# Attention scores of a two-layer transformer kernel: bf16 products of three parts against fp32 products in 32-row groups

## The chip, the core and the metric

The kernel runs on one core of a Trainium2 chip. The metric is the device time of one execution in microseconds (us). The engines are TensorE (PE in the profile, its weight loads PEld), VectorE (DVE), ScalarE (ACT), GpSimd (POOL) and SyncE (SP, which only issues DMAs here).

## The reference

1024 tokens of width 256 pass through two layers. Each layer is an attention and a mixture of experts, each with a LayerNorm ahead and behind and a residual. The change touches the two attentions alone (16 heads of width 16, causal):

```
q = x Wq (+ bq)    k = x Wk (+ bk)    v = x Wv (+ bv)      # the biases in layer 0; rotary q, k in layer 1
scores = q k^T * 16 ** -0.5 ;  scores[t, s] = -inf for s > t
y = softmax(scores) v ;  out = y Wo (+ bo)
```

The softmax subtracts from each row of scores its maximum, in the reference and in both kernels.

## The kernel before

Everything of the attention stays in SBUF. Queries are handled in two chunks of 512 tokens and keys in blocks of 128; heads go in four groups of four. For each layer the work goes so:

- **Head.** LayerNorm, transposes, then the projections (L624) give q and k as fp32 in X, transposed (channels on partitions). Scores need about fp32 accuracy, so each of q and k is split into three bf16 parts (L900 on ACT, L234 on DVE or POOL). SP copies them with 56 DMAs over both layers (L410), 16 rows at a time, to QA and KA: seven stacked products of 16 rows make 112 rows for each head. Rotary (layer 1) runs ahead of the split on DVE and POOL (L1116 to L1119, L536). The values (L635, with the bias as a product of one row, L638) go to V.
- **Maxima.** A *max unit* is a bank of PSUM with scores with queries on partitions: a bf16 product of 112 rows (L658), on the diagonal with a product of the constants `identb` and `mask_q` (L661) added to its last 128 columns, which puts -1e30 above the diagonal. DVE takes the maxima (L1134). Units of 128 columns hold four heads and those of 256 two. They use three banks in turn (`ps`, `RB = 3`), and a unit waits until DVE has emptied the bank (`unit_out`).
- **Rows.** The negated maxima in two bf16 parts (`nb`) are turned by TensorE (L667), copied by ACT (L941) and put by DMA into rows 112 and 113 of QA, against ones in KA. KA's ones come from a POOL memset (L524) at the start of each layer.
- **Scores.** 48 *steps* for each layer (group, query chunk, key block): four products with keys on partitions (L687, two heads for each ACT instruction), the exponential on ACT (L922), POOL's causal mask on diagonal blocks (L555), and *weigh*, four fp32 products with V side by side in 32 columns of the array each (L703). *Turn* turns the result (L673), DVE divides (L1151, L1152).

`schedule()` writes the order of units, scores and weighs by hand, and PE, ACT and DVE all follow it: each group's units stand between the scores of the group ahead. PE takes its instructions in that order.

Of the kernel before, what the change touches and what calls it, by code (L numbers as in the profile page):

```python
# [14 lines left out]
P = 128  # L15
# [21 lines left out]
Q_PARTS = (0, 0, 0, 1, 1, 1, 2)  # L37
K_PARTS = (0, 1, 2, 0, 1, 2, 0)
HM = H // KD
NPROD = 7  # L40
KQ = NPROD * DH
NSH = 2
KX = KQ + NSH
ONES_AT = KQ // 32 * 32

# [36 lines left out]
def max_units():  # L82


    units = []
    for i in range(NT):
        if i >= TPC:
            units += [(0, i, hh, 1, 0, CH) for hh in range(HG)]
# [3 lines left out]
    return units  # L92


MAX_UNITS = max_units()
NMAX = len(MAX_UNITS)
CHUNK_UNITS = [sum(u[1] < TPC * (c + 1) for u in MAX_UNITS) for c in range(NC)]
RB = 3
PB = 3

OWN_RATE, NEXT_RATE = 4, (5, 4, 4, 4)
OWN_AHEAD, NEXT_AHEAD = 10, 10
ROWS_AT = (6, NSTEP - 2)


def schedule():

    rest = [("max", 0, u) for u in range(CHUNK_UNITS[0], NMAX)] + [("rows", 0, 1)]
    out = [("max", 0, u) for u in range(CHUNK_UNITS[0])] + [("rows", 0, 0)] + rest[:OWN_AHEAD]
    rest = rest[OWN_AHEAD:]
    last = NG * NSTEP
    for st in range(last + 2):
        g, s = divmod(st, NSTEP)  # L120
        if s == 0 and g + 1 < NG:
            nxt = [("max", g + 1, u) for u in range(NMAX)]
        more = []
        if g == 0 and s < TPC:
            more = rest[:OWN_RATE]
            rest = rest[OWN_RATE:]
            if s == TPC - 1:
                more += rest + nxt[:NEXT_AHEAD]
                nxt = nxt[NEXT_AHEAD:]
        elif g + 1 < NG:  # L130
            more = nxt[:NEXT_RATE[g]]
            nxt = nxt[len(more):]
        if g + 1 < NG:

            for c in range(NC):
                if s == ROWS_AT[c]:
                    more.append(("rows", g + 1, c))
        if s == TPC + 3 and g < NG:
            more.append(("turn", NC * g))
        if s == 3 and 0 < g < NG:  # L140
            more.append(("turn", NC * g - 1))
# [7 lines left out]
        out += more  # L149
    return out + [("turn", NC * NG - 1)]  # L150


SCHEDULE = schedule()
UNITS = [x for x in SCHEDULE if x[0] in ("max", "rows", "turn")]
UNIT_NO = {x: n for n, x in enumerate(UNITS)}

EMPTIED = [sum(y[0] != "rows" for y in UNITS[:n + 1]) for n in range(len(UNITS))]
ROWS_DONE = [sum(y[0] == "rows" for y in UNITS[:n + 1]) for n in range(len(UNITS))]

# [17 lines left out]


DVE_PARTS = ((0, 0), (0, 1))
POOL_PARTS = ((1, 0), (1, 1))  # L180
# [29 lines left out]
def build(nc, a, out):  # L210
    ctx = ExitStack()
    with ctx:
# [7 lines left out]
        def left(L, m, j, part):  # L220

            who, those = ("pool", POOL_PARTS) if (m, j) in POOL_PARTS else ("dve", DVE_PARTS)
            return S(f"left{part}_{who}"), len(those) * L + those.index((m, j)) + 1

        def max_rows(eng, L, g, c):
            for j in range(NSH):
                eng.dma_start(QA[KQ + j:KQ + j + 1, HG * g:HG * (g + 1), c * CH:(c + 1) * CH],
                              mT[HG * j:HG * (j + 1), c * CH:(c + 1) * CH]).then_inc(S(f"max_rows{L}_{c}"), 16)

        def take_part(eng, L, m, j, part):  # L230

            eng.wait_ge(S(f"parts_p{part}_{L}"), 2 * m + j + 1)
            q = qkf[:, j, m, :]
            eng.tensor_tensor(q if part == 1 else parts[:, j, m, 2, :], q, parts[:, j, m, part - 1, :], ALU.subtract)\  # L234
               .then_inc(left(L, m, j, part)[0], 1)

# [14 lines left out]
        identb = sb("identb", [P, P], BF16)  # L251
        mask_q = sb("mask_q", [P, P], BF16)
# [25 lines left out]
        QA = sb("QA", [P, H, T], BF16)  # L278
        KA = sb("KA", [P, H, T], BF16)
        X = sb("X", [P, 10240])  # L280

        qkf = X[:, 0:4096].rearrange("p (a m t) -> p a m t", a=2, m=KD)
        parts = X[:, 4096:10240].bitcast(BF16).rearrange("p (a m r t) -> p a m r t", a=2, m=KD, r=PARTS)
# [4 lines left out]
        swapped = V[:, :, :, :].rearrange("p a b c -> p (a b c)")[:, 0:2 * T].rearrange("p (a t) -> p a t", a=2)  # L288
        by_cos = V[:, :, :, :].rearrange("p a b c -> p (a b c)")[:, 2 * T:4 * T].rearrange("p (a t) -> p a t", a=2)
        rden = sb("rden", [P, 2, TPC, HG])  # L290
        mx = sb("mx", [P, 2, NT, HG])
        nb = sb("nb", [P, NT, NSH, HG], BF16)
        mT = sb("mT", [NSH * HG, T], BF16)

# [55 lines left out]
        def _(sp):  # L350
# [42 lines left out]
            for L in range(2):  # L393
# [38 lines left out]
                if L == 0:  # L432
                    zero_sums(0)
                    zero_sums(1)


                rest = INTER[L] - P

# [1001 lines left out]
```

## Time and profile before

| what | us |
|---|---|
| median of three runs | 1030.9 (1030.26 to 1034.15) |
| span of the profiled execution, first to last instruction | 1058.4 |
| layer 0: first projection to first score | 28.46 to 110.15 |
| layer 0: first score to last turn | 110.15 to 239.84 |
| layer 1: first projection to first score | 594.75 to 677.39 |
| layer 1: first score to last turn | 677.39 to 807.54 |

The profiled execution is known by its span alone; it is 27.5 us above the median. Rows are read so: a mean in ns is from the start of one instruction to its end, and matmuls overlap, so the time that one really adds is the distance of the starts. An fp32 product is recorded as two passes, so a row "x8" can be four products.

### The profile page before, as it was taken

The page shows a single profiled execution, that of the slowest core. Times are in us where ns is not written, and L with a number is a line of the kernel's source. Part 1 is how long each engine was busy: PE and PEld are TensorE (multiplying, and loading weights), DVE is VectorE, ACT ScalarE, POOL GpSimd, SP SyncE. Part 2 cuts the span into 40 slices and gives each one's busy share as a digit, 9 for nine tenths or more (in the row PEclk, how much of TensorE's full clock was granted, in tenths as well). Part 3 has the DMA queues.
Part 4 walks back from the last instruction along what each step waited for, and adds up shares of the span by engine and source line. Part 5 has one row for each costly group of instructions (what it writes and reads, how often), then busy time and mean ns, then how long its engine had stood idle before and what let it go on. Part 6 is the DMA issues. An engine that isn't in the chain of part 4 may idle for free.

```text
span 1058.4 us, 14617 instructions
## 1 busy us (share of the span) xinstructions
PE 754.7 (71%) x4353; PEld 439.7 (42%) x4353; DVE 494.6 (47%) x1442; ACT 330.7 (31%) x660; POOL 336.4 (32%) x371
## 2 busy tenths in 40 slices
PE   0930899996753889999881632589998496899970
PEld 0510334423521667666660321134434443576650
DVE  7211977804630344444444762587742740144444
ACT  1500366682200222222220340246674320032221
POOL 6210011120075255555457150001110047035560
PEclk9965899999575899999995776799999598899995
DMA  2599053480052799999997099300000111089974
GB/s 74 60 115 103 2 167 103 147 264 1 1 177 77 227 246 261 270 260 262 247 231 212 2 118 119 40 12 2 2 1 22 67 48 41 24 235 264 263 178 129
DMA packets 88634, 134.28 MB, mean 127 GB/s; under 512 B 9883, under 2 KB 67082, under 8 KB 88464
## 3 DMA queue, kind: packets, MB, share of 16 engines
q1 hardware_dynamic: 57808, 101.31, 38.0%
q0 software_dynamic: 16896, 19.37, 10.6%
q10 hardware_dynamic: 13888, 13.06, 4.4%
q8 instruction: 24, 0.39, 0.2%
q14 instruction: 18, 0.15, 0.1%
HBM read 80.74 MB, written 40.06 MB: 114 GB/s over the span
## 4 chain that ended last, share of the span: by engine, by line
PE 29%; DVE 18%; POOL 14%; issue 14%; DMA 11%; another core or an unknown queue 5%; SPq 4%; ACT 4%; POOLq 0%; ACTq 0%; DVEq 0%
POOL acc L578 12%; DVE mx L1134 7%; DMA KA<-X 6%; PE ps L703 5%; PE ps L687 5%; PE ps L764 4%; SPq L410 4%; PE ps L658 4%; DMA acc<-X,token 3%; PE ps L798 2%; PE ps L605 2%; POOL pause L576 2%; ACT X L922 1%; PE ps L732 1%
## 5 line engine op out<-in xcount | busy, mean ns | idle before, releaser
L1134 DVE TENSOR_REDUCE mx<-ps 128x1 f32<-128x512 f32 (+3 forms) x304 | 180.2, 657 | 128.1 <-PE ps L661 76.7
L658 PE MATMUL ps<-KA,QA 112*128 112x512 bf16 (+3 forms) x384 | 116.7, 355 | 85.6 <-ACT mT L941 44.1
L922 ACT ACTIVATE X<-ps 128x1024 f32<-128x1024 f32 (+1 forms) x192 | 146.2, 811 | 84.9 <-PE ps L687 84.3
L578 POOL DMA_INDIRECT acc<-X,token x96 | 149.8, 1561 | 15.1 <-issue 14.9
L821 PE MATMUL ps<-X,KA 128*128 128x128 f32 x1152 | 149.3, 280 | 1.4 <-DMA KA<-in_ex 0.8
L821 PEld LDWEIGHTS ps<-X,KA 128*128 128x128 f32 x1152 | 139.6, 196 | 4.3 <-issue 2.9
L555 POOL TENSOR_SCALAR_AFFINE_SELECT X<-X 128x512 f32<-128x512 f32 x64 | 40.8, 637 | 311.2 <-ACT X L922 311.2
L1337 DVE TENSOR_SCALAR X<-ps,egate 128x256 f32<-128x256 f32 x96 | 46.5, 484 | 145.5 <-DMA acc<-X,token 145.0
L566 POOL DMA_INDIRECT slot_rows<-xn,slot_i x64 | 64.8, 1013 | 127.2 <-issue 73.7
L658 PEld LDWEIGHTS ps<-KA,QA 112*128 112x128 bf16 x384 | 37.4, 103 | 157.4 <-DVE mx L1134 50.8
L990 ACT ACTIVATE X<-ps 128x256 f32<-128x256 f32 x96 | 36.9, 385 | 201.9 <-DVE token L1311 84.2
L687 PE MATMUL ps<-QA,KA 114*128 114x512 bf16 (+3 forms) x384 | 92.7, 327 | 3.7 <-ACT X L922 3.4
L703 PE MATMUL ps<-X,V 128*32 128x512 f32 (+3 forms) x768 | 81.1, 497 | 0.4 <-ACT X L930 0.4
L605 PE MATMUL ps<-identf,xn 128*128 128x128 f32 x64 | 14.5, 415 | 89.1 <-ACT xn L866 72.3
L831 PE MATMUL ps<-KA,X 128*128 128x256 f32 x192 | 61.9, 404 | 22.3 <-DVE X L1326 10.3
L576 POOL TENSOR_TENSOR pause<-empty 128x1 f32<-128x1 f32 x96 | 20.1, 209 | 178.4 <-DVE X L1337 178.3
L764 PE MATMUL ps<-xT,w_sgu 128*128 128x512 f32 x112 | 59.5, 693 | 16.2 <-DVE QA L1221 8.2
L833 PE MATMUL ps<-KA,X 64*128 64x256 f32 (+1 forms) x192 | 67.6, 432 | 0.0
L798 PE MATMUL ps<-w_sdn,QA 128*128 128x256 f32 (+1 forms) x128 | 42.3, 474 | 25.8 <-issue 18.2
L661 PE MATMUL ps<-mask_q,identb 128*128 128x128 bf16 x256 | 54.7, 238 | 0.0
L605 PEld LDWEIGHTS ps<-identf,xn 128*128 128x128 f32 x64 | 12.7, 221 | 90.7 <-ACT xn L866 50.6
L687 PEld LDWEIGHTS ps<-QA,KA 114*128 114x128 bf16 x384 | 29.6, 98 | 48.3 <-ACT X L922 23.5
(174 smaller groups left out, 934.3 us busy)
## 6 DMA issues: line engine op xcount, KB each, us to landing
KA<-in_ex SPq DMA_DIRECT2D x96, 512.0 KB
slot_rows<-empty SPq DMA_DIRECT2D x12, 1060.0 KB, 10.1
X<-slot_rows ACTq DMA_DIRECT2D x96, 132.5 KB
QA<-X SPq DMA_DIRECT2D x28, 256.0 KB, 23.1
KA<-X SPq DMA_DIRECT2D x28, 256.0 KB, 25.4
KA<-in_dn SPq DMA_DIRECT2D x64, 64.0 KB
X<-acc SPq DMA_DIRECT2D x8, 512.0 KB, 6.6
acc<-empty SPq DMA_DIRECT2D x2, 1152.0 KB, 10.4
```

Source lines behind the costliest of these rows:

```text
L566: pool.indirect_dma_start(out=slot_rows[L], out_offset=bass.IndirectOffsetOnAxis(ap=slot_i[:, n:n + 1], axis=0), in_=xn[:, i, :], in_offse ...
L578: pool.indirect_dma_start(out=acc[L][r % 2], out_offset=bass.IndirectOffsetOnAxis(ap=token[:, r:r + 1], axis=0), in_=erows[:, r % 2, :], i ...
L658: mm = pe.matmul(ps[:, bank, j * w:(j + 1) * w], QA[0:KQ, h, i * P:(i + 1) * P], KA[0:KQ, h, s0:s0 + w], start=True, stop=not diag)
L687: mm = pe.matmul(ps[:, 4 + 2 * p + x, off:CH], KA[0:KX, h, b * P:(b + 1) * P], QA[0:KX, h, c * CH + off:(c + 1) * CH], start=True, stop=True)
L703: mm = pe.matmul(ps[32 * x:32 * x + 32, RB, off:CH], V[:, b, HG * g + x, :], probs[:, st % PB, x, off:CH], start=(b == 0), stop=(b == TPC ...
L764: mm = pe.matmul(ps[:, 2 * (u % 2) + x, :], w_sgu[:, k, col:col + P], xT[:, k, n * CH:(n + 1) * CH], start=(k == 0), stop=(k == KD - 1))
L798: mm = pe.matmul(ps[:, 6 + i % 2, 0:D], actv[0:rows_j, j, i * P:(i + 1) * P], w_sdn[0:rows_j, j, :], start=(j == 0), stop=(j == nsc - 1))
L821: mm = pe.matmul(ps[:, 2 + r % 2, m * P:(m + 1) * P], w_ex[:, r, col:col + P], rowsT[:, r % 2, k, :], start=(k == 0), stop=(k == KD - 1))
L831: pe.matmul(ps[:, 4 + r % 2, 0:D], eact[:, r % 2, 0:P], w_ex[:, r, KD * UPC * P:EW], start=True, stop=False)
L833: mm = pe.matmul(ps[:, 4 + r % 2, 0:D], eact[0:erest, r % 2, P:2 * P], w_rest[0:erest, r, :], start=False, stop=True)
L922: nc.scalar.activation(probs[:, st % PB, 2 * p:2 * p + 2, off:CH], ps[:, 4 + 2 * p:6 + 2 * p, off:CH], ACT.Exp, scale=SCALE).then_inc(S(f" ...
L1134: v.tensor_reduce(mx[:, part, i, h0:h0 + nh], ps[:, n % RB, 0:nh * w].rearrange("p (h w) -> p h w", h=nh), AX.X, ALU.max)\
```

## The change

- q and k are kept as fp32 in `QT` and `KT` (one buffer, QK), one plane for each group of four heads: head h of a group sits in partitions 32h to 32h+15. The weights' columns are arranged so that the projection puts group 2m into place; ACT writes k multiplied by a 0/1 column (`half`), with ones in the unused rows, and group 2m+1 comes from a DVE shuffle of partitions (`shuf`). The three parts, the 56 row copies and the memset of KA are gone.
- Every score is an fp32 product of 16 rows (maxima) or 17 (scores). The negated maximum of each query and head is written by DVE into `shifts`, TensorE turns it, and DVE adds it to row 16 of each head in QT (`rows`); the two DMAs for each of these are gone.
- A max unit now holds one head: 192 for each layer. Units come in pairs (heads 0,1 or 2,3), and a pair stands behind the score pair of the two other heads. On the diagonal the bf16 mask product of all 128 rows follows each unit's product. DVE takes plain maxima, one for each unit.
- Projections of the later heads and the values stand between the first group's max units. Layer 1's rotary is done in eight pieces of 512 columns.
- SP issues layer 0's later loads and the clearing of HBM at the start. POOL clears `shifts` and V's padding at the start.

The core of the diff:

```diff
-        w = (i % TPC + 1) * P
-        n = {1: 4, 2: 2, 3: 1, 4: 1}[w // P]
-        units += [(1, i, hh, n, (i // TPC) * CH, w) for hh in range(0, HG, n)]
+    for i in range(TPC * c, TPC * (c + 1)):
+        out += [(i, s0, CH) for s0 in range(0, CH * c, CH)] + [(i, CH * c, (i % TPC + 1) * P)]
...
+            out.extend(("max", g, i, 2 * side + x, s0, w) for x in range(2))
...
         for p in range(2):
             if st < last:
                 out.append(("score", st, p))
-            out += more[:1]
-            more = more[1:]
+            take(1 - p)
...
-                sp.wait_ge(S(f"k_ones{L}"), 1)
-                            for r in range(NPROD):
-                                if those[r] == part:
-                                    sp.dma_start(dst[DH * r:DH * (r + 1), HM * m:HM * (m + 1), :],
-                                                 parts[:, j, m, part, :]).then_inc(S(f"qa_rows{L}_{m}"), 16)
...
-                pool.memset(KA[ONES_AT:KX, :, :], 1.0).then_inc(S(f"k_ones{L}"), 1)
...
-                            mm = pe.matmul(ps[:, bank, j * w:(j + 1) * w], QA[0:KQ, h, i * P:(i + 1) * P],
-                                           KA[0:KQ, h, s0:s0 + w], start=True, stop=not diag)
-                            if diag:
-                                mm = pe.matmul(ps[:, bank, (j + 1) * w - P:(j + 1) * w], identb[:, :], mask_q[:, :],
-                                               start=False, stop=True)
+                        at = slice(32 * h, 32 * h + DH)
+                        mm = pe.matmul(ps[:, bank, 0:w], QT[at, g, i * P:(i + 1) * P], KT[at, g, s0:s0 + w],
+                                       start=True, stop=not diag)
+                        if diag:
+                            mm = pe.matmul(ps[:, bank, w - P:w], identb[:, :], mask_q[:, :], start=False, stop=True)
...
-                        mm = pe.matmul(ps[:, 4 + 2 * p + x, off:CH], KA[0:KX, h, b * P:(b + 1) * P],
-                                       QA[0:KX, h, c * CH + off:(c + 1) * CH], start=True, stop=True)
+                        at = slice(32 * (2 * p + x), 32 * (2 * p + x) + KS)
+                        mm = pe.matmul(ps[:, 4 + 2 * p + x, off:CH], KT[at, g, b * P:(b + 1) * P],
+                                       QT[at, g, c * CH + off:(c + 1) * CH], start=True, stop=True)
...
+                            v.tensor_reduce(shifts[:, c, i % TPC, at:at + 1], ps[:, bank, 0:w], AX.X, ALU.max,
+                                            negate=True).then_inc(S(f"unit_out{L}"), 1)
...
+                        v.scalar_tensor_tensor(q, q, half[:, 0:1], ps[:, bank, :], ALU.mult, ALU.add)\
                          .then_inc(S(f"unit_out{L}"), 1)
```

How the order of instructions changes is shown at three places. The first is PE between two weighs in layer 0. Before, L687 is a score product, L658 a max unit, L661 its mask, L703 a weigh:

```order
L687 MATMUL ps<-QA,KA 128x384 [waits exp0]
L687 MATMUL ps<-QA,KA 128x384
L658 MATMUL ps<-KA,QA 128x384 [waits unit_out0]
L661 MATMUL ps<-mask_q,identb 128x128
L687 MATMUL ps<-QA,KA 128x384 [waits exp0]
L687 MATMUL ps<-QA,KA 128x384
L658 MATMUL ps<-KA,QA 128x384 [waits unit_out0]
L661 MATMUL ps<-mask_q,identb 128x128
L703 MATMUL ps<-X,V 32x128 [waits masked0,exp0]
L703 MATMUL ps<-X,V 32x128 x3
```

The changed kernel at such a place, where L655 is a score product, L626 a max unit and L629 its mask:

```order
L655 MATMUL ps<-QK 128x512 [waits exp0]
L655 MATMUL ps<-QK 128x512
L626 MATMUL ps<-QK 128x512 [waits unit_out0]
L629 MATMUL ps<-mask_q,identb 128x128
L626 MATMUL ps<-QK 128x512 [waits unit_out0]
L629 MATMUL ps<-mask_q,identb 128x128
L655 MATMUL ps<-QK 128x512 [waits exp0]
L655 MATMUL ps<-QK 128x512
L626 MATMUL ps<-QK 128x384 [waits unit_out0]
L629 MATMUL ps<-mask_q,identb 128x128
L626 MATMUL ps<-QK 128x384 [waits unit_out0]
L629 MATMUL ps<-mask_q,identb 128x128
```

Two units, each with its own mask, now stand behind every score pair, where one stood. The second place is PE at the end of layer 0's head before; L635 and L638 are the values:

```order
L635 MATMUL ps<-w_qkv,xT 128x256 [waits qk_sb0]
L635 MATMUL ps<-w_qkv,xT 128x256
L638 MATMUL ps<-bias_v,ones_row 128x256
L658 MATMUL ps<-KA,QA 128x128 [waits qa_rows0_0]
L661 MATMUL ps<-mask_q,identb 128x128
```

And the changed kernel; L604 is a projection, L610 and L613 are the values:

```order
L604 MATMUL ps<-xT,w_qkv 128x512 [waits xT_dve]
L604 MATMUL ps<-xT,w_qkv 128x512 x3
L626 MATMUL ps<-QK 128x128 [waits head_sb0]
L629 MATMUL ps<-mask_q,identb 128x128
L626 MATMUL ps<-QK 128x128
L629 MATMUL ps<-mask_q,identb 128x128
L610 MATMUL ps<-w_qkv,xT 128x256 [waits head_sb0]
L610 MATMUL ps<-w_qkv,xT 128x256
L613 MATMUL ps<-bias_v,ones_row 128x256
```

The first unit waited for the row copies (`qa_rows0_0`) behind all projections and values; now it waits for an ACT result (`head_sb0`) and stands ahead of the values. The third place is POOL at the start. Before:

```order
L509 AFFINE_SELECT before<-before 128x128
L513 AFFINE_SELECT upto<-upto 32x32 x2
L516 MEMSET empty 128x1 [waits pool_own]
L524 MEMSET KA 18x16384 [waits consts]
L234 TENSOR_TENSOR X<-X 128x1024 [waits parts_p1_0,k_ones0]
```

The changed kernel:

```order
L498 MEMSET V 128x128
L500 AFFINE_SELECT before<-before 128x128
L504 AFFINE_SELECT upto<-upto 32x32 x2
L507 MEMSET pause 128x4 [waits pool_own]
L530 AFFINE_SELECT X<-X 128x4x128 [waits exp0,consts]
```

The memset of KA and POOL's share of the splitting are gone.

## Rows read from the trace of the kernel before

**Rows 1.** The page: busy time of the engines, and the chain that ended last.
```profile
PE 754.7 (71%) x4353; PEld 439.7 (42%) x4353; DVE 494.6 (47%) x1442; ACT 330.7 (31%) x660; POOL 336.4 (32%) x371
...
PE 29%; DVE 18%; POOL 14%; issue 14%; DMA 11%; another core or an unknown queue 5%; SPq 4%; ACT 4%; POOLq 0%; ACTq 0%; DVEq 0%
```

**Rows 2.** Windows, core 0: stretch, length, busy (count) by engine, clock, DMA share, GB/s.
```profile
28.46:110.15 81.69, 40.13 (x138) 19.52 (x138) 16.93 (x27) 16.20 (x25) 10.33 (x6) 0.71 0.82 90
110.15:239.84 129.69, 119.81 (x906) 47.15 (x904) 85.78 (x166) 80.41 (x111) 20.38 (x32) 0.99 0.46 139
594.75:677.39 82.64, 33.95 (x122) 18.61 (x121) 39.78 (x43) 16.76 (x26) 20.79 (x10) 0.71 0.80 89
677.39:807.54 130.15, 120.17 (x906) 47.63 (x904) 85.87 (x166) 80.41 (x111) 20.38 (x32) 0.99 0.01 4
213.00:239.84 26.84, 24.02 (x192) 7.22 (x192) 1.36 (x4) 21.05 (x31) 5.73 (x9) 1.00 0.85 261
```

**Rows 3.** Timeline at the start: start, length, engine, line, operation, tiles, count.
```profile
5.01 13.75 POOL L524 MEMSET KA<- 18x16384 bf16 x1
...
6.17 12.62 DVE L1045 TENSOR_SCALAR rs_sq<-mv 128x4 f32<-128x4 f32 x1
...
28.46 15.24 PE L624 MATMUL ps<-xT,w_qkv 128*128 128x512 f32 x32
```

**Rows 4.** Timeline of PE in layer 0's head, then the chain, then the first score.
```profile
45.12 1.13 PE L635 MATMUL ps<-w_qkv,xT 128*128 128x256 f32 x4
46.19 0.69 PE L638 MATMUL ps<-bias_v,ones_row 1*128 1x256 f32 x2
46.81 1.13 PE L635 MATMUL ps<-w_qkv,xT 128*128 128x256 f32 x4
...
72.40 32.81 DMA KA<-X
...
110.15 0.60 PE L687 MATMUL ps<-QA,KA 114*128 114x512 bf16 x2
```

**Rows 5.** Timeline of PE in layer 1's head.
```profile
599.47 7.03 PE L624 MATMUL ps<-xT,w_qkv 128*128 128x512 f32 x16
...
642.38 0.29 PE L658 MATMUL ps<-KA,QA 112*128 112x128 bf16 x1 [19.29 <-DMA KA<-X]
```

**Rows 6.** Groups by form: line, operation, shapes, count, busy, mean ns, idle before.
```profile
L1134 DVE TENSOR_REDUCE mx<-ps 128x1 f32<-128x512 f32 x192 | 120.1, 684 | 53.2 <-PE ps L658 51.1 <-PE ps L661 2.1
...
L922 ACT ACTIVATE X<-ps 128x1024 f32<-128x1024 f32 x96 | 93.7, 1026 | 61.6 <-PE ps L687 61.6
...
L661 PE MATMUL ps<-mask_q,identb 128*128 128x128 bf16 x256 | 54.7, 238 | 0.0
...
L1134 DVE TENSOR_REDUCE mx<-ps 128x1 f32<-128x384 f32 x64 | 32.1, 552 | 3.6 <-PE ps L661 3.6
...
L922 ACT ACTIVATE X<-ps 128x256 f32<-128x256 f32 x32 | 11.4, 384 | 10.7 <-PE ps L687 10.5
...
L673 PE MATMUL ps<-identf,X 128*128 128x128 f32 x64 | 10.0, 279 | 2.0 <-ACT X L930 1.6 <-DVE mx L1134 0.4
...
L1119 DVE TENSOR_TENSOR X<-V 128x1024 f32<-128x1024 f32 x4 | 9.0, 2253 | 0.1
...
L1116 DVE STREAM_SHUFFLE V<-X 128x1024 f32<-128x1024 f32 x4 | 5.2, 1304 | 0.0
```

**Rows 7.** Timeline of PE in layer 1's attention.
```profile
702.92 0.22 PE L661 MATMUL ps<-mask_q,identb 128*128 128x128 bf16 x1
703.07 1.06 PE L703 MATMUL ps<-X,V 128*32 128x512 f32 x8
704.07 0.82 PE L658 MATMUL ps<-KA,QA 112*128 112x512 bf16 x3
```

**Rows 8.** Timeline of PE among the experts.
```profile
470.33 0.70 PE L833 MATMUL ps<-KA,X 64*128 64x256 f32 x2
470.95 0.44 PE L809 MATMUL ps<-identf,X 128*128 128x128 f32 x2
```

More of the change, by code:

```diff
@@ L79 @@
 NSTEP = len(STEPS)
[L82 to L88, printed above, removed]
-        w = (i % TPC + 1) * P
-        n = {1: 4, 2: 2, 3: 1, 4: 1}[w // P]
-        units += [(1, i, hh, n, (i // TPC) * CH, w) for hh in range(0, HG, n)]
[L92 to L97, printed above, removed]
+NPROJ = 2 * KD * NC
+NVP = NT // 2
@@ L106, with take, take_behind, take_rows @@
-ROWS_AT = (6, NSTEP - 2)
+AHEAD = 6
+EXTRA = 2
 def schedule():
-    rest = [("max", 0, u) for u in range(CHUNK_UNITS[0], NMAX)] + [("rows", 0, 1)]
-    out = [("max", 0, u) for u in range(CHUNK_UNITS[0])] + [("rows", 0, 0)] + rest[:OWN_AHEAD]
-    rest = rest[OWN_AHEAD:]
+    first, rest = head_items()
+    out = list(first)
+    units = [(g, c, *u) for g in range(NG) for c in range(NC) for u in max_units(c)]
+    of = [sum((a, b) <= (g, c) for a, b, *_ in units) for g in range(NG) for c in range(NC)]
+    at = [0, 0]
+    rows = [0]
+    def take(side):
+        if at[side] < len(units):
+            g, _, i, s0, w = units[at[side]]
+            out.extend(("max", g, i, 2 * side + x, s0, w) for x in range(2))
+            at[side] += 1
+    def take_behind():
+        take(0 if at[0] < at[1] else 1)
+    def take_rows(least=0, beyond=1):
+        while rows[0] < NG * NC and (min(at) >= min(of[rows[0]] + beyond, len(units)) or rows[0] < least):
+            while min(at) < of[rows[0]]:
+                take_behind()
+            out.append(("rows", *divmod(rows[0], NC)))
+            rows[0] += 1
+    out += [("rope", 0), ("kmask", 0), ("rope", 1)]
+    while min(at) < of[0]:
+        take_behind()
+        if sum(at) == 2:
+            out += [("rope", 2), ("kmask", 2)]
+        if sum(at) == 4:
+            out.append(("rope", 3))
+        if rest:
+            out.append(rest.pop(0))
+    out += [("shuf", u) for u in (1, 0, 3, 2)]
+    for _ in range(AHEAD):
+        take_behind()
+    take_rows(1)
@@ L120, in schedule @@
         g, s = divmod(st, NSTEP)
[L121 to L141, printed above, removed]
+        if st < 4:
+            out.append(("rope", 4 + st))
+        if st in (1, 3):
+            out.append(("kmask", 3 + st))
+        if st in (4, 5):
+            out.extend(("shuf", u) for u in ((5, 4) if st == 4 else (7, 6)))
+        if st < last and s in (0, TPC):
+            take_rows(NC * g + (s == TPC) + 1)
         for p in range(2):
@@ L488, in _ @@
                               allow_small_or_imprecise_dtypes=True))
-            for t in (identf, identb, mask_q):
-                ch.step(pool.memset(t[:, :], 0.0))
+            for t in (identf, identb, mask_q, shifts):
+                ch.step(pool.memset(t[:], 0.0))
             for t in (before, ones, ones_row):
@@ L1094, in xT_copy @@
                     v.tensor_copy(xT[:, k, CH:T], ps[:, KD + k, :]).then_inc(S("xT_dve"), 1)
+            for odd in range(2):
+                ch.step(v.memset(half[:, odd:odd + 1], float(odd)))
+            ch.wait()
+            for odd in range(2):
+                for x in range(HG):
+                    v.memset(half[32 * x:32 * x + DH, odd:odd + 1], float(1 - odd)).then_inc(S("half"), 1)
             halves = (list(range(0, TPC)), list(range(TPC, NT)))
@@ L1126, in _ @@
[L1126 removed]
+                if L == 0:
+                    dve.wait_ge(S("consts"), 1)
+                    dve.wait_ge(S("half"), 2 * HG)
+                    dve.wait_ge(S("bias_qkv"), 32)
+                    ch.link(v.tensor_scalar(k_bias[:, 0, :], bias_qk[:, 1, :], half[:, 0:1], half[:, 1:2], ALU.mult, ALU.add))
+                    v.tensor_scalar(k_bias[:, 1, :], bias_qk[:, 1, :], half[:, 1:2], half[:, 0:1], ALU.mult, ALU.add)\
+                     .then_inc(S("k_bias"), 1)
```

427 lines of the change are left out of this document (211 added, 216 removed).

## The prediction, made before the changed kernel ran

> **What bounds the kernel now.** I read the windows first. From the first score to the last turn each layer takes 130 us, and PE is busy 120 of them, DVE 86, ACT 80 [rows 2]: TensorE bounds the loop, and only in its last 27 us, where no max units are left, ACT (21 of 26.8). Ahead of each loop stand 82 us between the first projection and the first score, with PE busy 40 and 34 of them, the DMA engines at 0.8 and the granted clock at 0.71 on average [rows 2]. The chain says why: the row copies hold the first max unit (17 to 19 us of idle) and the first row of maxima (32.81 us) [rows 4, 5]. Third, at the very start a DVE instruction on 4 columns takes 12.62 us and ends when POOL's memset of KA does (5.01 + 13.75) [rows 3]. Over the span PE is busy 71%, and it has the largest share of the chain, 29% [rows 1]. So the change can win in the heads and must pay in the loops. The experts are left as they are; I take nothing there.
>
> **Prices on TensorE.** A bf16 product of 512 columns takes 0.215 (three in 0.82, the last with its drain) and one of 128 columns 0.053 [rows 7]. An fp32 product runs as two passes of 0.43 (16 passes in 7.03 with the last one's drain) [rows 5]: 0.86 for 512 columns, four times as long. What the change counts on is that products in different parts of the array share this time. In columns they do: four fp32 weighs, eight passes, take 1.00 from start to start of the next work, 0.86 of it streaming [rows 7]. No row shows it for rows of 32; I take the same, pairs and quartets in the time of one.
>
> The other price is the change of the array's layout. From the mask to the weigh is 0.15, of which 0.053 is the mask: 0.10 for the switch; the weigh's 1.00 holds 0.10 for the switch back and 0.03 for weights [rows 7]. Products of 1 or 64 rows show the same for rows, and something more: two passes of 256 columns should take 0.43 and take 0.62, 0.19 more, a switch of 0.10 and a first fp32 weight load of 0.10 that nothing covers [rows 4, 8]. With this in hand the mask is dear: it needs all 128 rows, so behind each product of 16 rows come a switch, the mask, a switch, and an exposed weight load, 0.35 us instead of 0.053. It also parts the two units of a pair, which then don't overlap.
>
> **The loop, for each layer,** counted from the order of the changed kernel (first score onward):
> - Scores: 9 times 512 columns for each head, 16 heads in pairs: 72 x 0.86 = 61.9.
> - Max units on the diagonal: 108, together 69 times 512 columns, one by one: 59.3. Off it 56 in 28 pairs: 24.1.
> - Covered: the unit behind a score pair is on other rows and runs beside it. That is the shorter of the two at 45 diagonal pairs (19.4) and at 21 others (15.1): minus 34.5. Streams: 110.8.
> - Weighs 36 x 0.86 + 48 x 0.03 = 32.4. Masks 108 x 0.053 = 5.7. Switches 299 x 0.096 = 28.7 (96 before). First fp32 loads 132 x 0.10 = 13.2. Turns and rows 15 x 0.5 = 7.5 (four transposes are 0.28 each, overlapped [rows 6], plus a load).
>
> Sum 198. The same count for the kernel before gives 110, and 129.7 were measured: 20 of waits. Waits after: the last 15 steps go exp, score, weigh in a chain (1.03 for a full exp, 0.38 for the narrowest [rows 6], against 0.86 and 0.21 of streaming), 4; a pair of full units off the diagonal occupies DVE 2 x 0.684 [rows 6] with three banks, so the second of the next pair comes late, 28 x 0.4 = 12; the first group's second `rows` is wanted at once by the scores behind it, 3. That is 217. In layer 1 four rotary pieces (a shuffle of 0.65 and two of 1.1, from half of the rows of 1024 columns [rows 6]) stand in DVE's queue in the first steps ahead of the reduces, which PE waits for: 5 more, 222. Against 129.7 and 130.2: **87 + 92 = 179 lost.** The bounds: with all loads covered and no waits but the chain's, 185 in each layer (114 lost); with waits growing as the work does, 240 (220 lost).
>
> DVE has no say in this: plain maxima for one head each cost it, for 128 and 256 columns, about 0.29 and 0.42 (0.552 and 0.684 at 384 and 512 [rows 6], straight on down) instead of a shared 0.69, some 10 us for each layer, and the rows on DVE 8 x 0.7. It is then busy 102 of 217. ACT does less than before.
>
> **The heads.** Layer 0: without the memset the 12.62 is about 0.2, and the first projection starts at 16.5 instead of 28.46; POOL's new clearing of `shifts` and V stands near that DVE instruction but is short (bounds 9 to 12.4 gained). Four projections, partly at the low clock, 8.4; then between the 16 first units the values (8 x 1.69 from start to start [rows 4]) 13.5, four projections 6.9, the units themselves 10 x 0.86 and 16 x 0.35 = 14.2. That is 59.5. DVE's four shuffles and the 12 units ahead (8 x 0.684, 4 x 0.29) 9.2, the turned rows and their addition 1.5: first score at 70 instead of 110.15, **40 gained.** Layer 1: 594.75, rotary of the first keys and queries 9, values 8 x 1.07 [rows 4], 6.9 and 14.2 as above, 1.5 for full banks during a rotary piece, 9.2 and 1.5: first score at 646 instead of 677.39, **31 gained.** SP's loads and clearing that moved to the start stand behind w_qkv in its queue and delay nothing that I see; if they slowed it, by some 5 us, since the first projection comes 12 earlier.
>
> On the memset, the Trainium skill's SBUF — State Buffer (the table's "shared port pair") says that DVE and GpSimd take a port by exclusive lock for a whole instruction; the equal ends in the trace agree. Were it chance, 12 us of the gain would be gone.
>
> **Sum:** 179 - 71 = 108 slower. The profiled execution would go from 1058.4 to 1166; the median of the runs, 27.5 under its span, from 1030.9 to **1139**.
>
> **The rivals.**
> 1. *TensorE goes past the mask.* If a product on other rows could run beside a mask in another bank, with no drain, the row groups would be full: (123.8 + 59.3 + 48.2) / 4 = 58, with 32 + 6 + 7.5 103, and DVE's 102 and its waits would bound: 146 as a loop, 33 lost, 71 gained, 992. For: each waits for banks of its own. Against: the weigh, also in a bank of its own, pays 0.10 on either side [rows 7]. It decides below 165 for a loop. 10%.
> 2. *Row groups share less than column groups.* No row prices it; between full sharing (110.8) and none (231, see 3) I take a quarter of the way, 30 for each layer, 60 in all: 1200. Against: the weigh's 0.86, where four share fully [rows 7]. 12%. A page is for it: the Trainium skill, TensorE: Matmul & The Clock Gate ("Measured speedup vs the span model"), gives 3.07 times for four row tiles of 512 columns. By it the sum would be some 66 more.
> 3. *They don't share at all:* 231 instead of 110.8, 1380. Or the clock stays at its lower level (1.2 of 2.4 GHz) as in the heads before, where PE was idle half of the time [rows 2], though PE is now full: near 1500. Together 9%.
> 4. The sum as it stands, with the bounds above: 1139 + (114 - 179) = 1074 to 1139 + (220 - 179) = 1180. 69%.
>
> **How the numbers follow.** The forecast is rival 4's 1139. The range 1065 to 1215 takes in 4 and 2. Under 0.5% (5 us) a measurement of this kernel can't tell from no change. Rival 1 gives faster (0.10); 0.02 for a loop near 165; the rest, 0.88, is slower.
>
> **What would show it.** In the windows from first score to last turn: 217 and 222 with PE busy nearly throughout, DVE around half. A mask starts 0.10 after the end of its product's passes, and the next product of 16 rows pays 0.20; a score pair and the unit behind it start within a few ns. First scores near 70 and 31 us earlier than now in layer 1's own time; no 12-us DVE instruction at the start. I am wrong if the second unit of a diagonal pair starts beside the first, if a pair takes 2 x 0.86, or if the granted clock falls in the loop.

## The result, and the profile after

The changed kernel takes a median of 1400.9 us (1393.45 to 1424.68), the kernel before 1031.4 (1030.26 to 1034.15) beside it. The ratio is 1.355, with a 95% interval of 1.347 to 1.363. It is slower, as forecast, but by 369.5 us instead of 108, and outside the range. The profiled execution has a span of 1398.9. Single runs of one kernel that lie over 1.5% above its fastest, at a lower granted clock, are left out of every ratio and every comparison here.

The page of the changed kernel: busy time of the engines, PE's and the clock's rows over 40 slices, and the chain that ended last by engine and by line.

```profile
PE 1214.0 (87%) x5121; PEld 580.2 (41%) x5121; DVE 515.9 (37%) x1558; ACT 322.6 (23%) x632; POOL 289.9 (21%) x364
...
PE   6999999999995739898881999999999996899881
...
PEclk9855555555567669999995865555555566899996
...
PE 64%; POOL 12%; issue 11%; DVE 6%; DMA 4%; ACT 2%; POOLq 0%; ACTq 0%; DVEq 0%
PE ps L626 22%; PE ps L655 14%; POOL acc L553 9%; PE ps L671 9%; PE ps L629 4%; PE ps L744 3%; DMA acc<-X,token 2%; PE ps L604 2%; POOL slot_rows L541 2%; PE ps L778 2%; PE ps L610 1%; PE ps L580 1%; POOL pause L551 1%; PE ps L637 1%; PE ps L712 1%
```

PE's share of the chain went from 29% [rows 1] to 64%. The row to see is PEclk: it stands at 5 all through the middle of both loops, in slices in which PE is at 9, while in two slices near 1250 us, among the experts, PE is at 9 as well and the clock is at 9. In its loops TensorE is busy 99% of the time (92% before) and is granted half of its clock. Before, it was the other way round: 0.99 in the full loops and 0.71 in the half idle heads [rows 2].

The windows of the changed kernel: head of layer 0 (first projection to first score), its loop (first score to last turn), and the same for layer 1. Columns as in [rows 2], the clock third from the end.

```profile
16.51:74.37 57.86, 55.54 (x161) 25.17 (x161) 18.52 (x41) 10.92 (x16) 0.00 (x0) 0.85 1.01 276
74.37:420.04 345.67, 342.57 (x1264) 116.71 (x1264) 103.05 (x197) 80.58 (x104) 20.29 (x32) 0.53 0.00 1
769.16:823.52 54.36, 49.81 (x146) 23.90 (x145) 28.36 (x57) 11.25 (x17) 7.83 (x6) 0.85 0.00 0
823.52:1167.12 343.60, 340.63 (x1263) 116.22 (x1264) 110.69 (x212) 83.49 (x108) 22.82 (x34) 0.53 0.00 1
```

Against [rows 2] and [rows 3]: the start gained 12.0, the heads 23.8 and 28.3, and the loops lost 216.0 and 213.5. The rest of the span, almost all of it in code that the change leaves alone, is 24.9 shorter (580.9 for 605.8). That is the difference of 340.5 between the two spans. The 24.9 are the excess of the one profiled execution of before (27.5 above the median): another execution of nearly the same kernel (e8 below) has 580.8 there, as has the changed kernel. They are no gain of the change.

The timeline of PE in the changed kernel, on the diagonal in layer 0.

```profile
202.60 0.80 PE L655 MATMUL ps<-QK 17*128 17x256 f32 x2
202.61 0.79 PE L626 MATMUL ps<-QK 16*128 16x256 f32 x1
203.19 0.64 PE L655 MATMUL ps<-QK 17*128 17x256 f32 x2
203.20 0.63 PE L626 MATMUL ps<-QK 16*128 16x256 f32 x1
203.76 0.29 PE L629 MATMUL ps<-mask_q,identb 128*128 128x128 bf16 x1
203.98 1.22 PE L626 MATMUL ps<-QK 16*128 16x256 f32 x2
205.13 0.29 PE L629 MATMUL ps<-mask_q,identb 128*128 128x128 bf16 x1
205.35 0.80 PE L655 MATMUL ps<-QK 17*128 17x256 f32 x2
```

A score pair and the unit behind it, three fp32 products on three groups of rows, start within 0.01 us and take 1.16 together (202.60 to 203.76). The second unit alone takes 1.15 (203.98 to 205.13). So rows share fully, and the mask does part the pair, both as forecast. But 256 columns in two passes should stream in 0.43 and here need about twice that: every line of it is at the lower clock (0.50; the loop's mean is 0.53).

### The profile page after: what moved, and what is told of

Read it like the earlier page. It is cut to its first block, busy times and chain, and to the rows that moved or that the text cites. A ratio compares the mean times of both kernels' runs of the same rounds, so it can differ in the third digit from the quotient of the medians.

```text
span 1398.9 us, 16147 instructions
## 1 busy us (share of the span) xinstructions
PE 1214.0 (87%) x5121; PEld 580.2 (41%) x5121; DVE 515.9 (37%) x1558; ACT 322.6 (23%) x632; POOL 289.9 (21%) x364
## 4 chain that ended last, share of the span: by engine, by line
PE 64%; POOL 12%; issue 11%; DVE 6%; DMA 4%; ACT 2%; POOLq 0%; ACTq 0%; DVEq 0%
PE ps L626 22%; PE ps L655 14%; POOL acc L553 9%; PE ps L671 9%; PE ps L629 4%; PE ps L744 3%; DMA acc<-X,token 2%; PE ps L604 2%; POOL slot_rows L541 2%; PE ps L778 2%; PE ps L610 1%; PE ps L580 1%; POOL pause L551 1%; PE ps L637 1%; PE ps L712 1%
## 5 line engine op out<-in xcount | busy, mean ns | idle before, releaser
L626 PE MATMUL ps<-QK 16*128 16x512 f32 (+3 forms) x768 | 455.1, 864 | 6.1 <-DVE mx L1136 3.0
L655 PE MATMUL ps<-QK 17*128 17x512 f32 (+3 forms) x768 | 259.2, 853 | 5.3 <-DVE QK L1150 3.5
L1141 DVE TENSOR_REDUCE shifts<-ps 128x1 f32<-128x256 f32 (+3 forms) x256 | 125.4, 491 | 311.0 <-PE ps L629 310.7
L626 PEld LDWEIGHTS ps<-QK 16*128 16x128 f32 x768 | 158.4, 292 | 108.8 <-issue 55.0
L801 PE MATMUL ps<-X,WR 128*128 128x128 f32 x1152 | 149.6, 281 | 0.8 <-ACT X L962 0.7
L801 PEld LDWEIGHTS ps<-X,WR 128*128 128x128 f32 x1152 | 139.3, 195 | 4.3 <-issue 1.2
L1136 DVE TENSOR_REDUCE mx<-ps 128x1 f32<-128x512 f32 x128 | 83.5, 687 | 102.9 <-PE ps L626 102.7
L629 PEld LDWEIGHTS ps<-mask_q,identb 128*128 128x128 bf16 x256 | 26.0, 102 | 226.5 <-issue 225.6
L655 PEld LDWEIGHTS ps<-QK 17*128 17x128 f32 x768 | 89.6, 293 | 69.7 <-issue 31.1
L811 PE MATMUL ps<-WR,X 128*128 128x256 f32 x192 | 61.7, 403 | 28.0 <-DVE X L1331 27.6
L629 PE MATMUL ps<-mask_q,identb 128*128 128x128 bf16 x256 | 71.2, 278 | 0.0
L813 PE MATMUL ps<-WR,X 64*128 64x256 f32 (+1 forms) x192 | 66.9, 428 | 0.0
```

The lines of the kernel that those rows point to most:

```text
L626: mm = pe.matmul(ps[:, bank, 0:w], QT[at, g, i * P:(i + 1) * P], KT[at, g, s0:s0 + w], start=True, stop=not diag)
L629: mm = pe.matmul(ps[:, bank, w - P:w], identb[:, :], mask_q[:, :], start=False, stop=True)
L655: mm = pe.matmul(ps[:, 4 + 2 * p + x, off:CH], KT[at, g, b * P:(b + 1) * P], QT[at, g, c * CH + off:(c + 1) * CH], start=True, stop=True)
L801: mm = pe.matmul(ps[:, 2 + r % 2, m * P:(m + 1) * P], w_ex[:, r, col:col + P], rowsT[:, r % 2, k, :], start=(k == 0), stop=(k == KD - 1))
L813: mm = pe.matmul(ps[:, 4 + r % 2, 0:D], eact[0:erest, r % 2, P:2 * P], w_rest[0:erest, r, :], start=False, stop=True)
L1136: v.tensor_reduce(mx[:, i, h:h + 1], ps[:, bank, 0:w], AX.X, ALU.max, negate=True)\
```

## The experiments

Three explanations of the clock stood against each other. **A**: it follows how many of the array's 128 rows the products use, 16 or 17 in the changed loop against 112 and 114 before. **B**: the many changes between row groups and the whole array (299 for each loop) hold it down. **C**: it is the fp32 passes. I compare the loops, first score to last turn, by the same two stretches as above; what these experiments change lies there, but for some microseconds in the heads (first scores of the changed kernel and its variants come at 62 to 81).

**e1, 32 rows.** The products take in rows 16 (or 17) to 31 of each head too, and nothing else changes, not even the instructions' number. In the scores these rows hold ones against zeros and add nothing. In the maxima they hold ones against the queries of another group's head: that adds one number to a whole row of scores, shifts its maximum, and the softmax takes it out again.

```diff
-                        at = slice(32 * h, 32 * h + DH)
+                        at = slice(32 * h, 32 * h + 32)
...
-                        at = slice(32 * (2 * p + x), 32 * (2 * p + x) + KS)
+                        at = slice(32 * (2 * p + x), 32 * (2 * p + x) + 32)
```

> The changed kernel with 32 rows in every score and max product instead of 17 and 16; all else, the order, the layouts and the switches, stays. Theory A (the granted clock stays at its lower level because the products of few rows leave most of the array's rows idle): the clock rises in the loops, and at 2.4 GHz a loop is near 217 us instead of 345, the whole near 1140; if 32 rows are only partly enough, in between. Theory B (the clock stays low because of the switches of the array's layout, 299 in a loop): nothing moves, 1401 within 10. Theory C (because the passes are fp32): nothing moves either. The maxima then hold a part of other heads' queries, a shift that the softmax takes out again.

Measured: 1259.0, the mean of 1259.71 and 1258.23 (the median of all four runs is 1269.6, up to 1283.11), against 1033.6 for before on that chip. Its two loops:

```profile
80.30:353.40 273.10, 268.34 (x1264) 98.59 (x1264) 102.19 (x197) 80.10 (x104) 20.30 (x32) 0.72 0.00 1
751.40:1022.50 271.10, 265.09 (x1264) 98.29 (x1264) 109.50 (x212) 83.01 (x108) 23.10 (x34) 0.73 0.00 1
```

The same 1264 matmul passes in the same order, 72 us less in each loop, at 0.72 and 0.73 instead of 0.53. That speaks for A and against B and C, for which nothing was to move.

**e2, more work on 128 rows.** Two bf16 products of 128 rows and 512 columns ahead of the second unit of a diagonal pair, where PE has the whole array's layout anyway; the unit overwrites them.

```diff
+                        if diag and h % 2 == 1:
+                            for _ in range(2):
+                                pe.matmul(ps[:, bank, :], identb[:, :], fill[:, :],
+                                          start=True, stop=True)
```

> The changed kernel with two bf16 products of 128 rows and 512 columns added ahead of the second unit of each diagonal pair, into its bank, where the array is in the full layout already: 128 more products for each layer, no further switch. Theory A: the granted clock rises in the loops, and though work is added (64 x 0.43 = 27 us for each layer at 2.4 GHz) the time falls to about 1190. Theory B: the switches are the same, the clock stays, and at 1.2 GHz the added work costs 64 x 0.86 = 55 us for each layer: 1510. Theory C: between, nearer to B, since most of the time stays fp32.

Measured: 1486.1, ratio 1.442 [1.421, 1.463]. Layer 0's loop (e11's follow below):

```profile
76.80:465.70 388.90, 385.36 (x1371) 122.60 (x1372) 103.00 (x197) 80.65 (x104) 20.39 (x32) 0.53 0.00 1
```

The clock didn't move, and the time is nearer to B's 1510 than to A's 1190: a miss for A as I had put it. The loop is 43.2 longer: 54 x 2 x 0.215 is 23.2 at the full clock and 44 at 0.53. The added work was paid, at the low clock, and bought nothing. So I asked for more of it.

**e11, six of them instead of two** (range(6)).

> The changed kernel with six bf16 products of 128 rows and 512 columns, where the earlier filler had two, ahead of the second unit of each diagonal pair; its own products stay at 16 and 17 rows, the switches as they are. Two of them left the granted clock at 0.53 in the loops (1486 us). Theory A says that there was too little of the full layout: with six, the clock rises for much of the loop, 217 + 64 x 6 x 0.215 = 300 us at 2.4 GHz, the whole 1310 to 1450, less than with two although three times the work is added. If full products don't bring the clock back (then something of the 16-row products themselves holds it down), the loops go to 346 + 64 x 6 x 0.43 = 511 and the whole to 1730.

Measured: 1366.7, ratio 1.319 [1.299, 1.339].

```profile
80.60:407.40 326.80, 323.15 (x1588) 116.09 (x1588) 101.93 (x197) 80.25 (x104) 20.31 (x32) 0.82 0.00 1
814.60:1126.40 311.80, 306.70 (x1588) 112.22 (x1588) 109.53 (x212) 82.96 (x108) 22.82 (x34) 0.88 0.00 1
```

Three times e2's added work, and 119 us faster than e2 (on another chip; before takes 1036.1 there and 1033.6 on e2's); even below the changed kernel, which does none of it. Switches and fp32 passes are as many as in the changed kernel, so it isn't their number that holds the clock down. Their share of the time did fall, so this run alone doesn't rule out B and C; e4, e7 and e10 do. It also shows the mask at the full clock, in its timeline of PE:

```profile
206.52 1.12 PE L631 MATMUL ps<-QK 16*128 16x512 f32 x2
207.57 0.23 PE L634 MATMUL ps<-mask_q,identb 128*128 128x128 bf16 x1
207.73 0.42 PE L676 MATMUL ps<-X,V 128*32 128x128 f32 x8
```

From the unit's start to its mask 1.05, of which 0.86 stream; from the mask's start to the next product's, here a weigh, 0.16. Together 0.35 beyond the unit's streaming, the price in the prediction.

**e3, maxima over all 128 rows.** Each max unit now sums over all four heads of its group: its values are not one head's scores, and its rows can't be shared with another product.

```diff
-                        at = slice(32 * h, 32 * h + DH)
+                        at = slice(0, P)
```

> The changed kernel with its maxima over all 128 rows (the sum of four heads), so that they no longer share the array and the mask needs no switch; scores stay at 17 rows. Streams of maxima are 107 us for each loop instead of 49 beside the scores, at 2.4 GHz. Theory A: the clock is at 2.4 GHz for most of the loop, loops near 255, the whole near 1220, though the product work grew. Theory C (fp32): the clock stays low, loops near 480, 1680. Theory B (switches): about a third of the switches go, so the clock may rise in part, 1220 to 1500. The maxima are of the sum of four heads, not of each head.

Measured: 1232.2, ratio 1.195 [1.181, 1.210].

```profile
65.30:333.50 268.20, 264.11 (x1264) 104.07 (x1264) 105.56 (x197) 80.85 (x104) 20.39 (x32) 0.96 0.02 7
725.90:1005.40 279.50, 275.42 (x1264) 107.93 (x1264) 112.89 (x212) 83.55 (x108) 22.83 (x34) 0.91 0.00 1
```

This kernel gives up all sharing of the units and is 169 us faster than the one that has it. By the prediction's terms the units cost it 34.5 that nothing covers and 24.1 for unshared pairs; 217 + 58.6 is 276, with every switch left in. Some of them go, since mask and unit now have one layout (219 changes of layout in the trace of a loop, 299 before), and I had expected 255 at the full clock. Stretching what of that streams (149 + 58.6) to 0.96 and 0.91 gives an estimated 264 and 276; 268 and 280 came.

**e4, no mask product** (the maxima then run over keys above the diagonal too).

```diff
-                        diag = s0 + w == (i + 1) * P
+                        diag = False
```

> The changed kernel without the mask products in the maxima (they then take in later keys; the probabilities are still masked). All switches around masks go (216 of 299 in a loop) and the two units of a diagonal pair run beside each other. Theory A: rows are as few as ever, the clock stays at 1.2 GHz, and the time falls only by the work left out: 108 x about 0.5 and half of the diagonal streams (59), near 110 us for each layer, 1180. Theory B: with the switches gone the clock rises too, loops of 130 to 165, the whole at 970 to 1040.

Measured: 1220.8, ratio 1.184 [1.172, 1.197].

```profile
62.40:331.10 268.70, 265.06 (x1155) 109.39 (x1156) 99.81 (x197) 80.06 (x104) 20.30 (x32) 0.50 0.03 11
720.70:988.00 267.30, 261.41 (x1155) 106.38 (x1156) 106.93 (x212) 82.87 (x108) 22.85 (x34) 0.53 0.00 1
```

With 108 masks gone from each loop, the trace has 107 changes of layout there instead of 299, about as many as the kernel before (some 96) has at 0.99, and the clock is as low as it was. B falls for good. The masks cost 77 for each layer at this clock, less than the some 110 that I had put on them: where the two units of a pair can overlap, part of what they save goes elsewhere (see e6).

**e5, the masks of a pair together:** unit, unit, mask, mask, so that the pair overlaps and one visit to the whole array serves two.

```diff
+                        if diag and h % 2 == 0:
+                            return
                         if diag:
+                            pe.matmul(ps[:, (n - 1) % RB, w - P:w], identb[:, :], mask_q[:, :], start=False, stop=True)\
+                              .then_inc(S(f"unit{L}"), 1)
                             mm = pe.matmul(ps[:, bank, w - P:w], identb[:, :], mask_q[:, :], start=False, stop=True)
```

> The changed kernel with the two masks of a diagonal pair behind both products, not one behind each; rows stay at 16 and 17. The two units then run beside each other and half of the switches around masks go. If the price of the mask in my sum is right and the clock stays at 1.2 GHz: half of the diagonal streams at that clock (59) and 54 x about 0.5 us of switches, loads and masks' stops go, near 80 us for each layer, 346 to about 265, the whole near 1240. If the products with the same rows but denser raise the clock as well, less: 1100 to 1200. If the mask between the two cost nothing, 1401 stays.

Measured: 1259.0, ratio 1.217 [1.209, 1.225].

```profile
63.00:340.50 277.50, 272.93 (x1264) 104.90 (x1264) 98.83 (x197) 80.30 (x104) 20.30 (x32) 0.57 0.02 6
733.40:1026.60 293.20, 288.96 (x1263) 109.27 (x1264) 106.41 (x212) 83.32 (x108) 22.77 (x34) 0.52 0.00 1
```

68 and 50 us less for each loop with the work unchanged, where I had put 80: the second mistake of the changed kernel is the place of its masks.

**e6, e5 with 32 rows.**

> The two together: masks behind both products of a pair, and 32 rows in each score and max product. Theory A (the clock follows how much of the array's rows is in use): up to four products of 32 rows run at once for much of the loop, the clock is near 2.4 GHz there, a loop takes about 170 us and the whole about 1050. If the clock gets no higher than with 32 rows alone (0.72 in the loops), about 210 for a loop and 1130.

Measured: 1102.3, ratio 1.065 [1.060, 1.071], the best of the fp32 kernels that compute the whole. First its loops, then its PE around a step at the full clock (L659 scores, L626 units, L631 and L633 masks, L675 weigh):

```profile
62.80:267.40 204.60, 197.95 (x1264) 80.54 (x1264) 98.04 (x197) 80.05 (x104) 20.30 (x32) 0.88 0.02 7
660.60:871.90 211.30, 203.74 (x1263) 81.81 (x1264) 105.96 (x212) 82.97 (x108) 22.78 (x34) 0.85 0.00 1
```

```profile
180.14 0.70 PE L659 MATMUL ps<-QK 32*128 32x512 f32 x2
180.16 0.70 PE L626 MATMUL ps<-QK 32*128 32x512 f32 x2
180.68 0.59 PE L659 MATMUL ps<-QK 32*128 32x512 f32 x2
180.69 0.59 PE L626 MATMUL ps<-QK 32*128 32x512 f32 x2
181.22 0.23 PE L631 MATMUL ps<-mask_q,identb 128*128 128x128 bf16 x1
181.28 0.22 PE L633 MATMUL ps<-mask_q,identb 128*128 128x128 bf16 x1
181.43 0.70 PE L659 MATMUL ps<-QK 32*128 32x512 f32 x2
181.45 0.69 PE L626 MATMUL ps<-QK 32*128 32x512 f32 x1
181.97 0.59 PE L659 MATMUL ps<-QK 32*128 32x512 f32 x2
181.98 1.37 PE L626 MATMUL ps<-QK 32*128 32x512 f32 x3
183.28 1.06 PE L675 MATMUL ps<-X,V 128*32 128x512 f32 x8
```

Four fp32 products of 512 columns on four groups of rows take 1.08 from their start to the first mask, of which 0.86 stream: full sharing of four. The next quartet takes 1.85 (181.43 to 183.28): only one pass of a unit starts beside the scores' first passes, and the second unit is late. The row of its weight load says why:

```profile
182.23 0.29 PEld L626 LDWEIGHTS ps<-QK 32*128 32x128 f32 x2 [0.49 <-DVE shifts L1145]
```

It waited for DVE's reduce, that is for its bank, and from 182.23 on streams mostly alone. So overlap in row groups is lost when one of the four comes late, since PE keeps to its order. The loops of 205 and 211 are over the some 170 that I had expected at a high clock, though the clock came.

**e7, the kernel before with 16 rows.** The first of the seven stacked products alone, in maxima and scores, in bf16.

```diff
-                            mm = pe.matmul(ps[:, bank, j * w:(j + 1) * w], QA[0:KQ, h, i * P:(i + 1) * P],
-                                           KA[0:KQ, h, s0:s0 + w], start=True, stop=not diag)
+                            mm = pe.matmul(ps[:, bank, j * w:(j + 1) * w], QA[0:DH, h, i * P:(i + 1) * P],
+                                           KA[0:DH, h, s0:s0 + w], start=True, stop=not diag)
...
-                        mm = pe.matmul(ps[:, 4 + 2 * p + x, off:CH], KA[0:KX, h, b * P:(b + 1) * P],
-                                       QA[0:KX, h, c * CH + off:(c + 1) * CH], start=True, stop=True)
+                        mm = pe.matmul(ps[:, 4 + 2 * p + x, off:CH], KA[0:DH, h, b * P:(b + 1) * P],
+                                       QA[0:DH, h, c * CH + off:(c + 1) * CH], start=True, stop=True)
```

> The kernel before with only the first 16 of the 112 and 114 rows in its max and score products, still bf16; nothing else differs, neither the order nor the instruction count, but these products now are in another layout than masks and weighs, so that switches come in, about 200 in a loop, 20 us at most. Theory A: the granted clock falls in the loops though nothing is fp32 that was not, and the loops go from 130 to about 190 to 230 us, the whole to 1150 to 1230. Theory C (the fp32 passes): the clock stays, 130 plus 20, 1070. The scores then are products of the first bf16 parts alone, and the maxima are not subtracted.

Measured: 1243.1, ratio 1.202 [1.193, 1.211].

```profile
112.00:347.60 235.60, 232.74 (x905) 63.11 (x904) 93.16 (x165) 84.61 (x111) 20.29 (x32) 0.50 0.25 77
782.30:1015.80 233.50, 230.65 (x904) 62.82 (x904) 93.11 (x165) 84.61 (x111) 20.30 (x32) 0.51 0.01 2
```

The score products of the kernel before, bf16 and of the same columns, with fewer rows: the clock goes from 0.99 [rows 2] to 0.50, and 130 us become 235. C falls here. Part of the 105 is other: with 16 rows the masks and weighs stand on another layout, and the trace has some 305 changes of layout in a loop where I had reckoned with 200 (before has some 96). That such changes don't set the clock is what e4 showed.

**e9, the kernel before with 64 rows** (the same edit with 0:64).

> The kernel before with the first 64 of the 112 and 114 rows in its max and score products, where the run before it had 16 (that one came to 1243 us, its loops to 235 at a granted clock of 0.50). Order, instruction count and bf16 stay, and the switches to and from masks and weighs are as many as with 16 rows. Theory A (the clock follows the rows in use): loops at or near 2.4 GHz, 130 plus the switches (some 330 in a loop at 0.10, partly in waits), about 150 to 160, the whole near 1080. Theory B (the switches themselves keep the clock down): as with 16 rows, loops near 235, 1243. The scores then are products of four of the seven pairs of parts, and the maxima are not subtracted.

Measured: 1190.0 and 1152.3, on a chip on which before takes 1056.0. Both are above A's 1080 and under B's 1243. The profiled execution is the longer of the two, with a mean clock of 0.77 over the whole against 0.80 in the other, so the clocks below are if anything low.

```profile
111.50:246.00 134.50, 132.46 (x494) 37.29 (x494) 64.92 (x114) 43.29 (x56) 10.20 (x16) 0.50 0.18 53
246.00:308.30 62.30, 58.96 (x411) 19.90 (x410) 27.02 (x51) 40.23 (x55) 10.20 (x16) 1.00 0.62 175
748.70:939.10 190.40, 184.66 (x905) 56.41 (x904) 91.78 (x165) 83.37 (x111) 20.39 (x32) 0.69 0.01 2
```

0.66 (both stretches of layer 0 together) and 0.69 for the loops, between 0.50 at 16 rows and 0.99 at 112: in order, as A wants, but far from the nearly full clock that I had expected. Inside a loop the clock has one of its two levels, 0.50 for 134 us and 1.00 for the other 62. What tells the two stretches apart isn't settled; the second has fewer max units (48 passes in its 62 us against 114 in 134) and more of its passes are weighs, on 128 rows (208 of 411 against 176 of 494). At 64 rows the clock is thus not steady, and a mean such as 0.72 is a share of time, not a speed.

**e10, e4 with 32 rows:** no mask, the two differ in rows alone.

> The changed kernel with 32 rows in each product and without the mask products in the maxima (they take in later keys of the diagonal block; the probabilities are masked as ever). By theory A and my prices this is what the change would be without its two costs: 216 switches of 0.10 and their weight loads go from a loop, max and score pairs run four at once, the clock is near 2.4 GHz. PE then has 58 for scores and maxima, 32 for weighs, 13 for turns, rows and what switches are left: 120; DVE has 102. With waits 135 to 150 for a loop, and heads of 50: 1031 - 12 - 60 + 10 to 40, that is 970 to 1000, faster than the kernel before. If the clock stays at its lower level, 1150 or more.

Measured: 1074.0 against 1056.0 on that chip, ratio 1.016 [1.012, 1.021].

```profile
62.30:241.00 178.70, 170.68 (x1156) 75.57 (x1156) 96.80 (x197) 78.88 (x104) 20.30 (x32) 0.94 0.05 17
634.80:823.50 188.70, 179.89 (x1156) 79.28 (x1156) 104.86 (x212) 81.77 (x108) 22.83 (x34) 0.89 0.00 1
```

Rows alone take the clock from 0.50 and 0.53 (e4) to 0.94 and 0.89, and 90 and 79 us off the loops. But I had expected 970 to 1000, with loops of 135 to 150, and 179 and 189 came, at 0.94 and 0.89: some 30 too many. e6 is over its 170 by about as much. That late units break up quartets, as in the rows of e6, would do it. In layer 0's loop the units' weight loads stood behind DVE so (total us, times, longest):

```profile
PEld ps L626 <- DVE shifts L1141: 20.4, 33, 1.3
PEld ps L626 <- DVE mx L1136: 13.2, 20, 0.8
```

That is 33.6 us in 53 waits, with three banks for the units. How much of it lengthens the loop isn't shown; a run with more banks would show it, and there is none.

**e8, the kernel before with the memset of KA later:** POOL waits until both norms of the first chunk of rows are done.

```diff
+                if L == 0:
+                    pool.wait_ge(S("scaled"), 2)
                 pool.memset(KA[ONES_AT:KX, :, :], 1.0).then_inc(S(f"k_ones{L}"), 1)
```

> The kernel before with POOL's memset of KA in layer 0 held until DVE has computed both halves' first scales. If the memset is what holds the DVE instruction of 12.62 us, that falls to about 0.2, all of layer 0 starts 12 us earlier, and the time falls by 12 us, from 1031 to 1019 (the memset then ends near 24 us, before the row copies need it). If the 12.62 us have another cause, nothing changes.

Measured over six runs: 1021.9 (1014.29 to 1025.50) against 1034.9, ratio 0.986 [0.981, 0.990]. This kernel beats both. DVE, POOL and PE at its start:

```profile
6.24 0.17 DVE L1047 TENSOR_SCALAR rs_sq<-mv 128x4 f32<-128x4 f32 x1
...
12.32 13.75 POOL L526 MEMSET KA<- 18x16384 bf16 x1 [7.38 <-DVE shift L1066]
...
15.52 0.69 DVE L1096 COPY xT<-ps 128x512 f32<-128x512 f32 x1 [3.31 <-PE ps L607]
...
16.12 4.38 PE L626 MATMUL ps<-xT,w_qkv 128*128 128x512 f32 x6
```

The instruction of 12.62 us takes 0.17, the memset its 13.75 as before, and the first projection starts at 16.12 instead of 28.46. The two differ by the memset's place alone: it did hold DVE. And it doesn't hold every DVE instruction: the copy from PSUM at 15.52 lies in the middle of the memset and takes 0.69, as in the changed kernel, where no memset is near.

## Why the prediction was right in its sign and wrong in its size

**The step that failed** is in rival 3, second half: "the clock stays at its lower level ... as in the heads before, where PE was idle half of the time, though PE is now full". I read [rows 2] as the clock following PE's busy share, since it was 0.71 in half idle stretches and 0.99 in full ones, and so gave the case, with the one of no sharing, 9%. The rows fitted another reading as well: in those same full stretches nearly all of PE's products were of 112 to 128 rows. The changed loop has PE busy 99% and is granted 0.53; e7 has 99% and 0.50; e1 and e10 raise the clock by rows alone, e3 and e11 by work on all rows. Every price of the sum was taken from rows at the full clock, and so was applied at a clock that the kernel didn't have.

**The sum itself held, as far as this can be told.** The changed kernel and e1 have the same instructions at two clocks. If a loop is a part that stretches with the clock and one that doesn't, T = F + W / clock, layer 0 gives 345.7 and 273.1 at 0.53 and 0.72: W = 72.6 / (1.887 - 1.389) = 146, F = 70, and 216 at the full clock, where 217 was forecast; layer 1 (343.6 at 0.53, 271.1 at 0.73) gives 219 for 222. W is near the sum's streaming, 110.8 + 32.4 + 5.7 = 149. This extends a line of two points, one of them a mean over both levels, so its closeness is partly luck. But the same lines, with the fillers' streaming added to W, give e2's loop of layer 0 as 390 (388.9 measured) and e11's two as 333 and 318 (326.8 and 311.8), and e3's loops and the 0.35 in e11 don't rest on them at all. Of the 233 us by which the span passed the forecast, the loops have 250, the heads 7, and the rest of the span gave back 25. One bound was mis-summed, and nothing hangs on it: by its own terms the lower one of a loop is 198 - 13 + 4 = 189, not 185.

**Point by point.**
- Start: 12 forecast, first projection at 16.51 as written. e8 shows the cause. Here the Trainium skill (SBUF — State Buffer, the table's "shared port pair"), by which the loser of the port that DVE and GpSimd share is blocked for the other's whole instruction, agrees with the trace: DVE was held for what was left of the memset, 12.62 us.
- Heads: first score at 74.4 for 70; layer 1's head 54.4 for 51.3. Heads and start gained 64 for 71. The clock in them is 0.85; in e3, at 1.00 and 0.96, the heads are 48.8 and 45.5, so the missing 7 are the clock too.
- Full sharing of rows: right. The Trainium skill's TensorE: Matmul & The Clock Gate ("Measured speedup vs the span model") gives 3.07 for four row tiles; e6's quartet shows 4 in streaming time (0.86 for four products of 0.86), 3.2 with the switch and the first load counted (1.08), and less where a member is late. Rival 2 falls as put.
- The mask: right in price, 0.35 at the full clock (e11), and in that it parts the pair. I had it as 0.10 ahead of the mask and 0.20 behind; it is 0.19 ahead and, with the mask's 0.053, 0.16 behind. Rival 1 falls by the same rows.
- DVE: 103 busy for 102 forecast in layer 0, and no say in the time.
- Of the three signs by which I said I would be wrong, the third came: the granted clock falls in the loop.

Near 1500 for a low clock was itself too high by 100. Its working isn't written out; doubling what streams alone (149 for each loop) gives 1031 - 71 + 2 x (217 + 149 - 130) = 1432, and F above says that 70 to 80 us of each loop don't stretch.

## What to carry to other kernels

TensorE's speed is not told by its busy share: read the granted clock beside it for each stretch, and ask what the products there look like, not only how densely they stand. Where a change cuts a long loop's products to few rows, price it at both levels of the clock, and before anything else try the next wider slice whose extra rows add nothing or something that cancels, as e1 does: the same instructions were 142 us faster. A product on the whole array between products on row groups costs its switches and the group's overlap; put several such together (e5: also 142 us).

## What the runs showed of the hardware

- The granted clock in a full loop by rows used: 16 or 17 of 128, fp32 or bf16, 0.50 to 0.57; 32-row groups 0.72 and 0.73 (up to three at once), with paired units 0.85 to 0.94; 64 rows 0.66 and 0.69; 112 and 114 rows 0.99; maxima on 128 rows beside scores on 17 0.91 and 0.96. PE was recorded busy 92 to 99% in all of them. What about the rows sets the level isn't shown.
- Adding work can save time: 216 more products of 512 columns for each loop (e11 against e2) made the kernel 119 us faster.
- Products on four row groups start within 0.02 us and stream as one (e6: four of 0.86 in 0.86), if none of them waits for its bank.
- A POOL memset held an SBUF-to-SBUF DVE instruction on 4 columns for 12.62 us, and left a copy from PSUM at its 0.69.
